# Two cross attentions inside a decoder kernel: heads in row and column tiles, softmax by half sequences

## The reference, cut to what matters

```python
q = layernorm(x) @ Wq + bq ; k = ctx @ Wk + bk ; v = ctx @ Wv + bv      # 16 heads x 8
scores = einsum("bhqd,bhkd->bhqk", q, k) / sqrt(8)                      # 32 x 16 x 128 x 77
scores = where(mask == 0, -inf (first) or -1e9 (second), scores)
attn = softmax(scores, axis=-1)                                         # first: 0 where masked
x = x + einsum("bhqk,bhkd->bhqd", attn, v).reshape(...) @ Wout + bout
```

## Time and profile before

| | us |
|---|---|
| median of 3 runs | 3025.69 (3022.42 to 3032.64) |
| profiled execution | 3026.77 |
| its span, first to last instruction | 3025.0 |
| TensorE busy | 2610.4 (86%) |
| VectorE busy | 2333.7 (77%) |
| ScalarE busy | 1473.6 (49%) |
| GpSimd busy | 1452.5 (48%) |

### The profile page before, as it was taken

How to read it: one execution, slowest core, us unless ns; L and a number is a source line. 1 busy time by engine, 2 the same in 40 slices (tenths; PEclk the granted TensorE clock), 3 DMA queues, 4 the chain that set the end, 5 groups by cost and what they waited for, 6 DMA issues and landing times. The chain is left out here.

```text
span 3025.0 us, 44993 instructions
## 1 busy us (share of the span) xinstructions
PE 2610.4 (86%) x12704; PEld 1694.9 (56%) x12704; DVE 2333.7 (77%) x3947; ACT 1473.6 (49%) x2681; POOL 1452.5 (48%) x1216
## 2 busy tenths in 40 slices
PE   2888787788778767999879998799999899997997
PEld 0333333333333335666568887466666577775776
DVE  3999999999999986777545555588888699984555
ACT  3666676666667633444332222466666445442000
POOL 4666666666666766555510000455555566652000
PEclk8999999999999998999969999899999999997999
DMA  2000000000000001000000000000000100000000
GB/s 62 1 1 1 0 1 0 1 0 0 0 0 0 1 0 69 4 4 4 20 1 1 1 0 5 1 0 0 0 0 0 39 9 8 8 5 1 7 10 11
DMA packets 30806, 20.88 MB, mean 7 GB/s; under 512 B 18102, under 2 KB 29408, under 8 KB 30192
## 3 DMA queue, kind: packets, MB, share of 16 engines
q1 hardware_dynamic: 30704, 19.71, 2.3%
HBM read 17.60 MB, written 2.10 MB: 7 GB/s over the span
## 5 line engine op out<-in xcount | busy, mean ns | idle before, releaser
L783 POOL TENSOR_TENSOR m_hc<-m_h,m_cs 128x1024 f32<-128x1024 f32 x256 | 603.1, 2358 | 351.3 <-DVE m_h L705 346.7
L705 DVE TENSOR_TENSOR_SCAN m_h<-m_da,m_pdb 128x1024 f32<-128x1024 f32 x256 | 585.0, 2285 | 25.0 <-DVE m_pdb L660 6.8
L456 PE MATMUL m_py<-m_hc,ident 128*128 128x512 f32 x1024 | 513.7, 626 | 4.2 <-DVE m_y L669 2.1
L579 ACT ACTIVATE m_da<-m_dt,m_aneg 128x508 f32<-128x508 f32 x512 | 337.9, 709 | 46.1 <-POOL m_dt L752 44.4
L660 DVE TENSOR_TENSOR m_pdb<-m_du,m_pdb 128x1024 f32<-128x1024 f32 x256 | 314.7, 1229 | 39.6 <-POOL m_du L759 11.4
L456 PEld LDWEIGHTS m_py<-m_hc,ident 128*128 128x128 f32 x1024 | 201.6, 199 | 212.5 <-issue 174.0
L978 ACT ACTIVATE x_prT<-x_pt 77x512 f32<-77x512 f32 x256 | 151.8, 593 | 316.5 <-PE x_pt L894 316.5
L1121 POOL TENSOR_TENSOR x_pr<-x_pr,x_rden 128x308 f32<-128x308 f32 x256 | 179.4, 701 | 196.1 <-DVE x_rden L1043 195.4
L920 PE MATMUL x_py<-x_prT,x_va 77*32 77x128 f32 x2048 | 271.0, 276 | 0.0
L594 ACT ACTIVATE m_cs<-m_pc 128x512 f32<-128x512 f32 x256 | 150.5, 588 | 220.1 <-PE m_pc L446 220.1
L442 PE MATMUL m_pdb<-m_bcrow,m_sel 96*128 96x512 bf16 x256 | 102.5, 400 | 175.4 <-DVE m_h L705 174.4
(11 more groups left out here) (250 smaller groups left out, 5784.2 us busy)
## 6 DMA issues: line engine op xcount, KB each, us to landing
cw_gu<-in_C_gu SPq DMA_DIRECT2D x1, 2304.0 KB
x<-in_x SPq DMA_DIRECT2D x8, 256.0 KB, 5.5
fw_w<-in_F_w SPq DMA_DIRECT2D x1, 2048.0 KB
out_x<-x SPq DMA_DIRECT2D x8, 256.0 KB, 2.3
x_mrow<-in_B_mrow SPq DMA_DIRECT2D x1, 1232.0 KB, 6.0
x_ctxT<-in_B_ctxT SPq DMA_DIRECT2D x32, 38.5 KB, 1.8
x_ctxT<-in_E_ctxT SPq DMA_DIRECT2D x32, 38.5 KB, 1.8
x_mask<-in_E_mask SPq DMA_DIRECT2D x32, 38.5 KB, 1.8
```

Of the source, the lines that this page charges most:

```text
L456: ins = mm(py[:, c, :], S.ident[:, :], hc[n % BUF][:, place(n, c), :], start=n == 0, stop=n == NS - 1)
L579: A_(dst, src, ACT.Exp, scale=aneg[:, d, c, n:n + 1]).then_inc(s["da_ready"], 1)
L705: V.tensor_tensor_scan(h[n % BUF][:, way], da[n % BUF][:, d:d + CH * GT][:, way], pdb[:, b:b + 2, :].rearrange("p c t -> p (c t)")[:, way] ...
L783: P.tensor_tensor(hc[n % BUF][:, :, :], h[n % BUF][:, :].rearrange("p (c t) -> p c t", c=CH), bc(cs[n % BUF][:, :], 1, CH), ALU.mult).then ...
```

## The change

The walk is now over half sequences of eight heads (`Half`, `walk_halves`), so that softmax instructions handle 8 x 77 = 616 elements in each partition instead of 308, and there are half as many. A half's scores lie in two PSUM banks.

Scores: one masked copy `kd` of four heads' width serves all quads. Quad e's matmul reads the 32 rows of q and `kd` that hold its four heads, rows 32e to 32e+31. The two matmuls of a half stand in different row tiles and write different banks.

Masks: both stages add a bf16 tile `madd` (0 or -1e30) by TensorE, in the first stage with 32 rows of ones in the same row tile, in the second with the identity over 128 rows. The copy_predicated is gone. In the first stage `mrow` is loaded with the weights at the program's start.

Values: the sixteen matmuls of a sequence stand together, ordered so that four consecutive ones write to the four 32-wide column tiles; they come one sequence later, from four buffers `prT` per sequence.

Moved: the bias of v and the spreading into `va` from VectorE to GpSimd, v's copy out of PSUM to ScalarE, the memsets of `va` to GpSimd; the mean and variance are taken by VectorE (bn_aggr) and the power -1/2 by GpSimd one sequence at a time, where GpSimd did ten operations for 4 and then for 28 sequences.

```diff
+class Half:
+    def __init__(self, j, p, h):
+        self.seq = Seq(j, p)
+        self.n, self.p, self.h = self.seq.n, p, h
+        self.k = 2 * self.n + h
+    def plus(self, k):
+        b = self.seq.plus((self.h + k) // 2)
+        return Half(b.j, b.p, (self.h + k) % 2)
+    def real(self):
+        return self.seq.real()
+def walk_halves(eng, slot, ahead):
+    turns = (ahead + 1) // 2
+    def both(j):
+        for p in range(2):
+            for h in range(2):
+                slot(Half(j, p, h))
+    for j in range(-turns, 1):
+        both(j)
+    with eng.Fori(1, NB // 2 - turns) as j:
+        both(j)
+    for j in range(NB // 2 - turns, NB // 2 + 1):
+        both(j)
...
     W.hmask = W.tile("hmask", [128, HX], w["hmask"])
+    if not full_mask:
+        W.mrow = W.tile("mrow", [128, NB * TC], w["mrow"].partition_broadcast(128), I32)
...
+        kd = [A.sb(f"kd{p}", [128, QH, TC]) for p in range(2)]
...
+        pr = [[A.sb(f"pr{p}{h}", [128, H2, TC]) for h in range(2)] for p in range(2)]
+        prT = [[A.sb(f"prT{p}{q}", [TC, QH * T]) for q in range(NQ)] for p in range(2)]
...
+        ps = [A.ps(f"ps{h}", [128, Q2, 512]) for h in range(2)]
...
+        pyo = A.ps("pyo", [128, 512])
...
+                def turn(u):
+                    pe.wait_ge(s["norm_ready"], u.k + 1)
+                    for e in range(Q2):
+                        if due(Q2 * (u.k - 1) + e + 1):
+                            pe.wait_ge(s["prT_ready"], Q2 * (u.k - 1) + e + 1)
+                        for i in range(QH):
+                            ins = tr(pt[e][0:TC, i * T:(i + 1) * T], pr[u.p][u.h][:, QH * e + i, :], S.ident[:, :])
+                        ins.then_inc(s["pt_mm"], 1)
...
+                def scores(u):
+                    if u.h == 0:
+                        pe.wait_ge(s["q_ready"], u.n + 1)
+                        pe.wait_ge(s["kd_ready"], u.n + 1)
+                        pe.wait_ge(s["madd_ready"], u.n + 1)
...
+                    if due(u.k - 1):
+                        pe.wait_ge(s["sub_ready"], u.k - 1)
+                    for e in range(Q2):
+                        rows = slice(32 * (Q2 * u.h + e), 32 * (Q2 * u.h + e) + 32)
+                        mm(ps[u.h][:, e, 0:QK], qT[u.p][rows, :], kd[u.p][rows, :, :], start=True, stop=False)
+                    for e in range(Q2):
+                        rows = slice(32 * (Q2 * u.h + e), 32 * (Q2 * u.h + e) + 32)
+                        if full_mask:
+                            ins = mm(ps[u.h][:, e, 0:QK], S.ident_bf[:, :], bc(madd[u.p][:, :], 1, QH),
+                                     start=False, stop=True)
+                        else:
+                            ins = mm(ps[u.h][:, e, 0:QK], ones[rows, :], bc(madd[u.p][rows, :], 1, QH),
+                                     start=False, stop=True)
+                    ins.then_inc(s["s_mm"], 1)
...
+                def values(b):
+                    pe.wait_ge(s["prT_ready"], NQ * (b.n + 1))
+                    pe.wait_ge(s["v_ready"], b.n + 1)
+                    if due(b.n):
+                        pe.wait_ge(s["cT_ready"], b.n)
+                        pe.wait_ge(s["x_ready"], b.n)
                     for i in range(QH):
...
-                        ins = mm(py[b.p][W4 * q:W4 * q + W4, 0:T], va[b.p][:, q, W4 * i:W4 * i + W4],
-                                 prT[q % 2][:, i * T:(i + 1) * T], start=i == 0, stop=i == QH - 1)
+                        for q in range(NQ):
+                            ins = mm(pyo[W4 * q:W4 * q + W4, 0:T], va[b.p][:, q, W4 * i:W4 * i + W4],
+                                     prT[b.p][q][:, i * T:(i + 1) * T], start=i == 0, stop=i == QH - 1)
                     ins.then_inc(s["y_mm"], 1)
...
+                def project_out(b):
+                    pe.wait_ge(s["cT_ready"], b.n + 1)
+                    mm(pyo[:, T:2 * T], cT[:, :], W.wo[:, :], start=True, stop=True).then_inc(s["o_mm"], 1)
+                def slot(u):
+                    last = u.seq.plus(-1)
+                    if u.real():
+                        turn(u)
+                    if u.plus(2).real():
+                        scores(u.plus(2))
+                    if u.h == 0:
+                        if u.seq.plus(2).real():
+                            project_in(u.seq.plus(2))
+                        if last.real():
+                            values(last)
+                    else:
+                        if last.real():
+                            project_out(last)
+                        if u.seq.plus(3).real():
+                            turn_x(u.seq.plus(3))
...
+                def moments(lo, hi):
+                    for b in range(lo, hi):
+                        ins = V.bn_aggr(mv[:, b, :], S.bn[:, b, :])
+                    ins.then_inc(s["aggr"], 1)
+                    dve.wait_ge(s["aggr"], 1 if lo == 0 else 2)
+                    V.tensor_scalar(ve[:, lo:hi], mv[:, lo:hi, 1], LN_EPS, None, ALU.add).then_inc(s["ve_ready"], 1)
+                moments(0, EARLY)
...
+                moments(EARLY, NB)
+                if not full_mask:
+                    V.tensor_scalar(brow[:, :], W.mrow[:, :], 0.0, MASKED, ALU.is_equal, ALU.mult
+                                    ).then_inc(s["brow_ready"], 1)
...
+                def slot(u):
+                    d, a = u.plus(1), u.plus(2)
+                    m, n, o = u.seq.plus(2), u.seq.plus(3), u.seq.plus(-1)
+                    if d.real():
+                        dve.wait_ge(s["exp_ready"], d.k + 1)
+                        if due(d.k - 3):
+                            dve.wait_ge(s["rden_ready"], d.k - 3)
+                        V.tensor_reduce(den[d.p][d.h][:, :], pr[d.p][d.h][:, :, :], AX.X, ALU.add
+                                        ).then_inc(s["den_ready"], 1)
...
+                        sc = ps[a.h][:, :, 0:QK].rearrange("p e (i k) -> p e i k", k=TC)
+                        dve.wait_ge(s["s_mm"], a.k + 1)
+                        if due(a.k - 3):
+                            dve.wait_ge(s["sub_ready"], a.k - 3)
+                        V.tensor_reduce(top[a.p][a.h][:, :].rearrange("p (e i) -> p e i", i=QH), sc, AX.X, ALU.max
+                                        ).then_inc(s["top_ready"], 1)
...
+                        dve.wait_ge(s["den_ready"], d.k + 1)
+                        if due(d.k - 3):
+                            dve.wait_ge(s["norm_ready"], d.k - 3)
+                        V.reciprocal(rden[d.p][d.h][:, :], den[d.p][d.h][:, :]).then_inc(s["rden_ready"], 1)
+                    if u.h == 1 and o.real():
+                        dve.wait_ge(s["y_mm"], o.n + 1)
+                        if due(o.n):
+                            dve.wait_ge(s["o_mm"], o.n)
...
+                            V.tensor_scalar(cT[:, :], pyo[:, 0:T], some[:, bass.ds(o.n, 1)], None, ALU.mult
+                                            ).then_inc(s["cT_ready"], 1)
...
+                        dve.wait_ge(s["top_ready"], a.k + 1)
+                        if due(Q2 * (a.k - 3)):
+                            dve.wait_ge(s["pt_mm"], Q2 * (a.k - 3))
+                        V.tensor_tensor(pr[a.p][a.h][:, :, :].rearrange("p (e i) k -> p e i k", i=QH), sc,
+                                        bc(top[a.p][a.h][:, :].rearrange("p (e i) -> p e i", i=QH), 3, TC),
+                                        ALU.subtract).then_inc(s["sub_ready"], 1)
...
+                            dve.wait_ge(s["s_mm"], Q2 * (m.n - 1))
+                        V.tensor_scalar(madd[m.p][:, :], ints, 0.0, MASKED, ALU.is_equal, ALU.mult
+                                        ).then_inc(s["madd_ready"], 1)
...
+                def slot(u):
+                    d = u.plus(1)
+                    c, m, r = (u.seq.plus(k) for k in (1, 2, 4))
...
+                        pool.wait_ge(s["rden_ready"], d.k + 1)
+                        buf = pr[d.p][d.h]
+                        P.tensor_tensor(buf[:, :, :], buf[:, :, :], bc(rden[d.p][d.h][:, :], 2, TC), ALU.mult
                                         ).then_inc(s["norm_ready"], 1)
...
+                        if due(Q2 * (m.n - 1)):
+                            pool.wait_ge(s["s_mm"], Q2 * (m.n - 1))
+                        P.tensor_tensor(kd[m.p][:, :, :], bc(kT[:, :], 1, QH), bc(hm4[:, :], 2, TC), ALU.mult
                                         ).then_inc(s["kd_ready"], 1)
```

More of the change, by code:

```diff
@@ L884, in _ @@
                 pe.wait_ge(W.loaded, W.all())
[L885 to L892, removed]
-                    for i in range(QH):
[L894 to L910, removed]
@@ L961, in _ @@
+                walk_halves(pe, slot, 3)
             @block.scalar
@@ L997, in _ @@
+                walk_halves(act, slot, 3)
             @block.vector
@@ L1067, in slot @@
-                    if q == 1 and o.real():
-                        dve.wait_ge(s["y_mm"], NQ * (o.n + 1))
-                        if due(o.n):
-                            dve.wait_ge(s["o_mm"], o.n)
-                        y = py[o.p][:, 0:T]
```

(25 more changed lines are left out.)

282 lines of the change are left out of this document (97 added, 185 removed).

## The result

The changed kernel takes 3206.02 us (3203.79 to 3208.13, four runs) against 3024.89 (3022.42 to 3032.64): ratio 1.0594, 95% interval 1.0573 to 1.0615. It is 6% slower; 2936 was predicted, in a range that ended at 3014. From the last VectorE instruction of the stage ahead to its own last one, the first cross attention took 363.1 us before and takes 424.0, the second 318.4 and 435.0; the stages ahead of, between and behind them are the same within 1 us. So all of the loss lies where the change is.

What follows compares the result with a forecast made beforehand. TensorE bounded the kernel, VectorE close behind in the second stage; after the change, a ring of waits would. Savings of 74 and 16 us (90), less 1.1 for the profiled run, took 3026.8 to 2936 us; 8-in-10 range 2897 to 3014.

Steps and rivals of the forecast that it cites:

- rival 4: TensorE's clock, both cross attentions: waits in every half may halve it, adding about 1.9 us a half; chance 0.05.
- Its price for all halves at half clock, 3180: Both cross attentions: if every half ran at half clock, the kernel would take 3180 us.
- Values of four column tiles together: TensorE's value matmuls: four column tiles run at the same time, 0.87 us instead of 3.5 a sequence.
- rival 2: TensorE's value matmuls run two and two, 0.87 us more in half 0, giving 2962 us; chance 0.11.
- rival 3: TensorE's value matmuls: four column tiles do not overlap, block keeps 3.5 us, 139 us more, 3075; chance 0.04.
- both row tiles together: TensorE's scores: the two matmuls of a half run at the same time, 0.52 us instead of 1.04.
- rival 1: TensorE's scores: row tiles run one after another, 0.52 us more a half, 3010 us; chance wholly or half 0.16.
- normalisation 1.22: GpSimd's normalisation of a half, 616 elements, takes 1.22 us, extrapolated from 308 and 512 elements.
- the hand-over from the mask's end to VectorE: Between TensorE's mask matmul and VectorE's maximum: 0.04 us a half.
- the ring: Chain through VectorE, GpSimd and TensorE that each half goes round once: 4.22 us, 4.50 in the second stage.
- 8.44 and 9.00: Forecast us a sequence in the first and second cross attention, instead of 10.64 and 9.35.
- first stage 60 us less instead of 74, second 7.5 instead of 16: Forecast savings of 74 and 16 us: 32 sequences' shorter periods plus 4 and 4.4 us at the stages' starts.

Runs made afterwards that it cites:

- 3636.87: Kernel before, with its 128-row score matmuls taken on 32 rows (rows 0 to 31), one at a time: 3636.87 us.
- 3033.24: Changed kernel with score matmuls on all 128 rows instead of 32, scores not the reference's: 3033.24 us.
- 2963.63: Changed kernel plus nine bf16 matmuls a sequence (128x128 by 512) that nothing reads, placed where TensorE would wait: 2963.63 us.
- 3113.36: Kernel before plus two more VectorE maxima over the scores for each quad of heads, no tiles of the changed kernel: 3113.36 us.
- 3416.07: Kernel before plus five more VectorE maxima over the scores for each quad of heads, no tiles of the changed kernel: 3416.07 us.
- 3043.71: Changed kernel with scores on all 128 rows and the value matmuls one column tile after another: 3043.71 us.
- 3323.76: Changed kernel plus nine matmuls a sequence that nothing reads, each on one 32-row tile (32x128 by 512): 3323.76 us.

## Why the prediction was wrong

**The step that failed** is rival 4, the clock, held at 0.05 with the reason that "the clock fell behind 3 us in which TensorE was busy 1.05; here each wait is under 1 us". It treated the clock as a matter of gaps alone, and looked for a fall in the steady part. Nor were the gaps under 1 us: by the prediction's own times TensorE stands still some 1.2 us in half 1, and 1.3 were measured. The runs show two things in its place. The clock falls at the edge of the stage and has to rise out of half, before as after (0.50 from 1148 to 1163 us in both). And 32-row score matmuls keep it down even where TensorE never waits (0.50, 3636.87 us), while 128-row ones of the same place let it rise in spite of the waits (0.94, 3033.24). Neither is the whole: with 32-row scores and the waits filled by full-height matmuls the clock is full (2963.63), and with waits alone, on the kernel before, it is full or dips (3113.36, 3416.07). The prediction saw the row tiles only as a question of whether two run together. Its price for all halves at half clock, 3180, was 26 us short of what was measured.

**The rest of the mechanism** held once the clock was full. Values of four column tiles together (rival 2 and rival 3 fall), both row tiles together (rival 1 falls), normalisation 1.22, maximum 0.80, VectorE waiting for the scores: all as forecast. Mis-sized was the hand-over from the mask's end to VectorE, 0.12 us instead of 0.04; with small delays at the reciprocal and, in half 1, behind the fill, that makes the ring 4.33 and 4.41 in the two halves. By its normalisations the filled kernel has 8.75 and 9.22 us a sequence (46 starts from 1201.2 to 1398.0 us, 43 from 2402.3 to 2596.0) where 8.44 and 9.00 stood, and takes 2963.6 us where 2936 stood: first stage 60 us less instead of 74, second 7.5 instead of 16, and 4 us more outside the two.

**Rival 3's price** was too high too: column tiles one after another in the program cost 10 us, 3043.71 against 3033.24, not 139, since the block lasted 2.46 us and not 3.5. But the clock was 0.99 in one and 0.94 in the other, so part of the price is hidden in that.

**Left open:** how waits and 32-row matmuls add up in what the clock follows; why it comes up for a moment now and then in the changed kernel (some windows show 0.53, not 0.50); and what matmuls on 64 rows do to it.

## What to carry to other kernels

Read the granted clock of each stage before and after, and count a new operand shape as a change to the clock, not only to the cycles: matmuls that use 32 of the 128 rows can halve the clock of all their neighbours (0.50 in the run of 3636.87 us, 1.00 in the kernel before, with only the rows of the scores changed). Here both stages are at half clock at their start or within 4 us of it, behind a pause of TensorE (busy 3.75 of the 12.6 us from 2402.4 to 2415 in the kernel before), so ask what will bring it up. Where TensorE has time to spare, a few full-height matmuls that nobody reads can be worth having (four of them a sequence: 3206 to 2966 us). Cutting the ring of waits gave more than filling it: 2866 us, and 2846 with the mask made earlier and three fills.

## What the runs showed of the hardware

- Column tiles need not be interleaved in the program to overlap. With all eight instructions of a tile in a row, the next tile's began 0.467 us after the first of the one before, with five of its eight started, and the block lasted 2.46 us at full clock, where 3.5 was reckoned (timeline of the run of 3043.71).
- Four column tiles of 77x32 run fully together: 32 instructions start within 0.81 us at full clock (run of 2963.63), 1.52 at half (changed kernel).
- A matmul of 32 rows by 512 bf16 columns is as long as one of 128 rows (three in a row at full clock: 0.82 and 0.81 us, runs of 3323.76 and 2963.63), and does not keep the clock up as it does (0.53 and 1.00 from 1200 to 1350 us). An fp32 score matmul of 308 columns lasts 1.39 us at half clock on 32 rows (its two instructions, run of 3636.87), as against 1.40 on 128.
